# A one-core graph network kernel: the loads and the first of 16 batches in a new order, parameters worked out on GpSimd, the first neighbour product in single precision, and eight matmuls on zeros ahead of it

## The reference

```python
h = relu(bn(conv1d(xc, conv1_w, 0)))            # 1 tap, 128 -> 128 channels
h = bn(conv1d(h, conv2_w, 8))                   # 17 taps
x_conv = relu(h + xc)
s = x @ w_se.T + b_se                           # 3 columns
dist = sq[:, :, None] + sq[:, None, :] - 2 * einsum('bnd,bmd->bnm', s, s)
A = exp(-dist) * mask                           # mask is adj, 512 x 512
msg = relu(x @ w_msg.T + b_msg)
x_nmp = einsum('bnm,bmd->bnd', A, msg)          # the neighbour product
gi = concat([x_conv, x_nmp]) @ w_ih.T + b_ih;  gh = x @ w_hh.T + b_hh
r, z, n = sigmoid(..), sigmoid(..), tanh(gi_n + r * gh_n)
x = layernorm(x + (1 - z) * n + z * x)
```

## Time and profile before

| | us |
|---|---|
| median of 3 runs | 405.14 (403.12 to 405.31) |
| the profiled execution | 401.42 |
| its span | 399.1 |
| TensorE busy in the span | 374.6 (94%) |
| VectorE | 355.7 (89%) |
| ScalarE | 230.7 (58%) |
| GpSimd | 41.5 (10%) |

### The profile page before, as it was taken

One profiled execution on the slowest core, in us unless ns is written; L12 is line 12 of the kernel. 1 busy time (PEld: TensorE's weight loads), 2 busy tenths in 40 slices (PEclk: granted clock), 3 DMA queues, 4 the chain that ended last, 5 costly groups with the idle time before them and its releaser, 6 DMA issues.

```text
span 399.1 us, 7030 instructions
## 1 busy us (share of the span) xinstructions
PE 374.6 (94%) x2263; PEld 326.7 (82%) x2263; DVE 355.7 (89%) x731; ACT 230.7 (58%) x356; POOL 41.5 (10%) x46
## 2 busy tenths in 40 slices
PE   3589899999999999999999999999999999899995
PEld 2478689898979797989898898989797979688783
DVE  4988779999999999999999999999999999986646
ACT  4355456747565665666665667475656754654450
POOL 4500002110010101010101010100101060101013
PEclk9988889999999999999999999999999999999999
DMA  7627040504122221404040504040312204000100
GB/s 196 213 56 210 1 132 11 157 3 140 27 71 93 65 94 38 129 4 154 10 158 0 158 10 149 9 137 25 97 66 69 89 12 132 2 26 2 30 29 21
DMA packets 27305, 30.17 MB, mean 76 GB/s; under 512 B 3086, under 2 KB 16326, under 8 KB 27286
## 3 DMA queue, kind: packets, MB, share of 16 engines
q1 hardware_dynamic: 27256, 29.92, 24.5%
q10 hardware_dynamic: 30, 0.01, 0.0%
HBM read 24.84 MB, written 4.40 MB: 73 GB/s over the span
## 4 chain that ended last, share of the span: by engine, by line
PE 63%; DVE 21%; issue 10%; ACT 4%; DMA 1%; DVEq 0%; SPq 0%; POOLq 0%; ACTq 0%; POOL 0%
PE p_outer L602 14%; PE ring L602 13%; PE p_middle L602 8%; PE p_r L602 8%; PE p_z L602 8%; PE p_gi L602 7%; PE p_gh L602 4%; DVE sd_l L1121 3%; DVE dd L1107 2%; DVE sd L1116 2%; DVE st L1198 2%; DVE m_l L1130 2%; DVE n_l L1281 2%; DVE sd L1117 1%; ACT rows L840 1%
## 5 line engine op out<-in xcount | busy, mean ns | idle before, releaser
L602 PE MATMUL p_middle<-sd_h,w_h 128*128 128x256 f32 x192 | 56.7, 295 | 0.0
L1010 POOL TENSOR_TENSOR rs<-base,cst 128x5 f32<-128x5 f32 x16 | 20.0, 1250 | 332.7 <-DVE base L1209 332.7
L602 PE MATMUL p_middle<-sd_h,w_l 128*128 128x256 f32 x192 | 54.4, 283 | 0.0
L602 PE MATMUL p_middle<-sd_l,w_h 128*128 128x256 f32 x192 | 54.1, 282 | 0.0
L602 PE MATMUL p_outer<-dd_h,w_h 128*128 128x256 f32 x176 | 50.0, 284 | 2.5 <-issue 2.5
L865 ACT ACTIVATE am<-ring 128x512 f32<-128x512 f32 x64 | 37.9, 595 | 24.7 <-PE ring L602 24.3
L602 PE MATMUL p_outer<-dd_h,w_l 128*128 128x256 f32 x176 | 50.2, 285 | 0.0
L602 PE MATMUL p_outer<-dd_l,w_h 128*128 128x256 f32 x176 | 50.0, 284 | 0.0
L1136 DVE TENSOR_TENSOR am<-am,adj 128x512 f32<-128x512 f32 x64 | 40.9, 683 | 2.9 <-ACT am L865 2.9
L1252 DVE TENSOR_TENSOR am_l<-am,am_h 128x2048 fp32r<-128x2048 f32 x16 | 36.7, 2293 | 3.7 <-ACT am_h L914 3.7
L602 PEld LDWEIGHTS p_outer<-dd_h,w_h 128*128 128x128 f32 x176 | 34.0, 193 | 3.8 <-issue 3.2
(11 more groups left out here) (288 smaller groups left out, 969.7 us busy)
## 6 DMA issues: line engine op xcount, KB each, us to landing
adj<-adjT SPq DMA_DIRECT2D x64, 256.0 KB, 3.3
xin<-xT SPq DMA_DIRECT2D x17, 256.0 KB, 2.8
out<-yo SPq DMA_DIRECT2D x16, 256.0 KB, 2.2
gw<-g_w SPq DMA_DIRECT2D x2, 640.0 KB
wc<-w_c SPq DMA_DIRECT2D x2, 384.0 KB, 4.7
right<-left SPq DMA_DIRECT2D x14, 48.0 KB
wg<-w_ih SPq DMA_DIRECT2D x1, 384.0 KB, 5.8
wc<-w_c SPq DMA_DIRECT2D x1, 320.0 KB, 3.6
```

The lines of the kernel that those rows point to most:

```text
L602: return nc.tensor.matmul(out_, w, x, start=start, stop=stop, skip_group_check=True)
L1010: TT(rs[:], base[:], cst[:, C_MH:C_MH + CH + 1], ALU.pow).then_inc(s_rs, 1)
```

## The change

The pieces in front of the loop and step 0 become a function `first()` on TensorE, ScalarE and VectorE; the loop starts with step 1. What it does:

- SyncE's queue: the second batch's `xin` and the first third of `wc2` move ahead of `cst`; the loads of `bd` move from behind `xin` 2 to ahead of `bmsg`. ScalarE issues `vec`, `wc1` and `wrow` itself, ahead of its first instruction.
- GpSimd works out all of `prm` (10 small instructions; 14 were on VectorE, one on GpSimd). The two weight sums and `w4_l` go from GpSimd to VectorE. `right[1]` of the first pair is copied by a DMA instead of VectorE.
- TensorE runs eight matmuls of 128x512 on `right[0]`, just cleared, into `p_outer`, which is overwritten later.
- The neighbour product of batch 0 takes `am` and `m0` (relu of the messages, in the tile `zt`) as they are: 4 single-precision matmuls, no `am_h`, `am_l`, `m_h`, `m_l` for that batch.
- The four distance products of batch 0 have a bank each (`FIRST_D`). The identity is added to `sel1` on VectorE where it is read out of PSUM, not to `bd`.
- TensorE, ScalarE and VectorE have the same instructions otherwise, in another order.

```diff
             sp.dma_start(xin[:, 0, :], xT[0, :, :]).then_inc(s_x[0], 16)
-            sp.dma_start(wc1[:], w_c1[:, :]).then_inc(s_wc1d, 16)
-            sp.dma_start(vec[:], vecs[:, :]).then_inc(s_vec, 16)
+            sp.dma_start(xin[:, 1, :], xT[1, :, :]).then_inc(s_x[1], 16)
+            sp.dma_start(wc2[:, 0::3, :], w_c2[:, 0::3, :]).then_inc(s_w2d[0], 16)
             sp.dma_start(cst[:], consts[:, :]).then_inc(s_cst, 16)
...
+            def first():
+
+                pe.wait_ge(s_ready, 1)
+                for _ in range(8):
+                    mm(p_outer[:], right[0][:, 0:D], right[0][:])
+                pe.wait_ge(s_xh, 1); pe.wait_ge(s_w1s, 1)
+                mm(R_C1[:], wc1_h[:], x_h[0][:], True, False)
...
+                pe.wait_ge(s_left, 1); pe.wait_ge(s_right[0], 16); pe.wait_ge(s_h1, 1); pe.wait_ge(s_mt, 1)
+                for c in range(CH):
+                    mm(FIRST_D[c][:], left[:, D * c:D * c + D], right[0][:]).then_inc(s_d[c], 1)
...
+                pe.wait_ge(s_m0, 1); pe.wait_ge(s_mt, 2)
+                for c in range(CH):
+                    pe.wait_ge(s_am[c], 1)
+                    last = mm(R_NMP[:], m0[:, D * c:D * c + D], am[:, c, :], c == 0, c == CH - 1)
+                last.then_inc(s_nmp, 1)
...
+            def first():
+                act.dma_start(vec[:], vecs[:, :]).then_inc(s_vec, 16)
+                act.dma_start(wc1[:], w_c1[:, :]).then_inc(s_wc1d, 16)
+                act.dma_start(wrow[:, 64:128], w_rows[:, :]).then_inc(s_wrowd, 16)
+                z = Fixed(0)
+                x_high(0, z, 0)
+                x_high(0, z, 1)
+                act.wait_ge(s_zero, 3); act.wait_ge(s_prm, 5)
+                first_conv(z, 0)
...
+            pool.wait_ge(s_vec, 16); pool.wait_ge(s_zero, 1)
+            TS(prm[:, P_VE:P_VE + 2], vec[:, V_V1:V_V2 + 1:4], EPS, None, ALU.add).then_inc(s_prm, 1)
+            pool.wait_ge(s_prm, 1)
+            TT(prm[:, P_RS:P_RS + 2], prm[:, P_VE:P_VE + 2], half[:], ALU.pow).then_inc(s_prm, 1)
...
+            def first():
+                z = Fixed(0)
+                dve.wait_ge(s_wc1d, 16)
...
+                x_low(0, z, 1)
+                dve.wait_ge(s_brow, 32); dve.wait_ge(s_cst, 16)
+                TS(rowb[:], brow[:], cst[:, C_ROW:C_ROW + 1], cst[:, C_ROW + 1:C_ROW + 2], ALU.mult, ALU.add).then_inc(s_rowb, 1)
+                differences(z, 0)
...
+                TT(wsum[:, 0, 0:G3 - 1, :], wc2[:, 0:TAPS - 2:3, :], wc2[:, 2::3, :], ALU.add).then_inc(s_wsum, 1)
...
+                TT(w4_l[:], wc2[:, 2::3, :], full(w4_h[:]), ALU.subtract).then_inc(s_wlo, 1)
...
+                dve.wait_ge(s_bmsg, 16)
+                msg_sum(z, 0, FIRST_MSG)
...
+                TT(wsum[:, 1], wsum[:, 0], wc2[:, 1::3, :], ALU.subtract).then_inc(s_wsum, 1)
```

More of the change, by code:

```diff
@@ L216, in part @@
             return flat[0:rows, a:a + PAIRS * width].rearrange("p (j w) -> p j w", w=width)
-        sel1 = part(wc2, 0, 64, CC)
+        sel1 = [t[0:64, 0:4 * CC].rearrange("p (j w) -> p j w", w=CC) for t in (rt, nn)]
+        m0 = zt
         diag = part(wc2, 0, CC, CC)
@@ L479, in batches @@
         def batches(eng, step):
-            for b in (0, 1):
-                step(b, b, Fixed(b))
+            step(1, 1, Fixed(1))
             with eng.Fori(0, (B - 4) // 4) as i:
@@ L551, in _ @@
             sp.dma_start(xin[:, 2, :], xT[2, :, :]).then_inc(s_x[2], 16)
[L553 to L556, removed]
+            sp.wait_ge(s_left, 1)
+            sp.dma_start(full(right[1][64:64 + KD, :]), full(left[96:96 + KD, :])).then_inc(s_right[1], 16)
             for c in range(CH):
@@ L652, in transposes, with spread_rows @@
                 last.then_inc(s_t, 1)
-            def adjacency(stage):
+            def spread_rows():
                 sel = cst[0:64, C_SEL:C_SEL + CC]
[L657 to L667, removed]
-                            last = mm((p_gi, p_gh)[h][0:CC, CC * j:CC * j + CC], sel1[:, HP * h + j, :], sel)
-                        last.then_inc(s_acm, 1)
-                else:
-                    pe.wait_ge(s_ac, 2)
-                    for j in range(PAIRS):
-                        last = mm(p_middle[0:CC, j:j + 1], ac[0:CC, j, :], cst[0:CC, C_ONE:C_ONE + 1])
-                    last.then_inc(s_deg, 1)
+                pe.wait_ge(s_bdd, 32); pe.wait_ge(s_cst, 16); pe.wait_ge(s_val, 1)
+                for h in range(2):
+                    for j in range(HP):
+                        last = mm((p_gi, p_gh)[h][0:64, CC * j:CC * j + CC], bd[:, HP * h + j, :], sel)
+                    last.then_inc(s_sel1m, 1)
@@ new lines, in spread_columns, with degrees @@
+            def spread_columns():
+                sel = cst[0:64, C_SEL:C_SEL + CC]
+                pe.wait_ge(s_sel1, 2)
+                for h in range(2):
+                    for j in range(HP):
+                        last = mm((p_gi, p_gh)[h][0:CC, CC * j:CC * j + CC], sel1[h][:, j, :], sel)
+                    last.then_inc(s_acm, 1)
+            def degrees():
+                pe.wait_ge(s_ac, 2)
+                for j in range(PAIRS):
+                    last = mm(p_gi[0:CC, j:j + 1], ac[0:CC, j, :], cst[0:CC, C_ONE:C_ONE + 1])
+                last.then_inc(s_deg, 1)
@@ L932, in step @@
                     g_act.combined(act)
[L933 to L937 removed]
+                node_rows(n, -1)
+                conv_sums(n)
                 if more:
@@ L943, in step @@
                         g_act.channels(act, i)
-                after(act, s_cv, n(1)); after(act, s_gz, n(0))
-                A(c_h[:], cv[:], ACT.Relu).then_inc(s_ch, 1)
-                after(act, s_nmp, n(1)); after(act, s_gn, n(0))
-                A(n_h[:], R_NMP[:], ACT.Copy).then_inc(s_nh, 1)
+                conv_out(n)
+                neighbours(n)
                 if more:
                     exps(n, 1, 0)
-                after(act, s_gx, n(1)); after(act, s_tt, n(0))
-                A(gg[:], p_gh[:], ACT.Identity, bias=prm[:, P_HB:P_HB + 1], scale=0.5).then_inc(s_ghb, 1)
+                gate_n(n)
                 if more:
@@ L1279, in step @@
                     sums_low(n, 1)
[L1280 to L1292 removed]
+                neighbours_low(n)
+                conv_low(n)
+                normalise(q, n, -1, pair_of(b, v))
                 if more:
@@ L1303, in pair_of @@
                 return loop_pair[0] * 2 + (v - 1) // 2
-            for b in (0, 1):
-                step(b, b, Fixed(b))
+            first()
+            step(1, 1, Fixed(1))
             with dve.Fori(0, (B - 4) // 4) as i:
```

471 lines of the change are left out of this document (238 added, 233 removed).

## The result

The changed kernel takes 389.21 us (median of 4 runs, 387.48 to 390.19), the kernel before 405.23 beside it (4 runs, 403.12 to 406.61). The ratio is 0.9604, 95% interval 0.9550 to 0.9659: faster by 16.0 us. I had forecast 394.1 with a range of 390.5 to 399.0.

A forecast was written before the change was run, and what follows sets the result against it. With the loop unchanged and TensorE and VectorE nearly full, the second batch's earlier start was the whole effect. VectorE's terms, -4.3 - 0.6 - 4.2 + 3.4 - 4.8 - 0.1, gave -10.6, taken as -11: 405.14 to 394.1 us, range 390.5 to 399.

The forecast's parts named there:

- VectorE's shift is the smaller, so it decides: End of batch 0: VectorE's `gg` 11 us earlier, TensorE's step 1 13.1 earlier; the smaller shift reaches the end.
- The shift is the same for each: Whole time: the same 11 us come off the span, the profiled execution (401.42) and the median (405.14).
- The slow VectorE rows: VectorE, 9.75 to 16 us: three instructions slowed beside GpSimd's large ones return to 0.70 each, 4.3 us less.
- The rival that they stay slow: VectorE's 2 us instructions have another cause, such as loads, and stay slow: 401.5 us, chance 0.06.
- The instructions added and removed: VectorE in batch 0: 4.2 us less for instructions removed, 3.4 us more for those added.
- Idle time: VectorE from `rowb` to `gg`: walked 2.0 us of waits, took 3.0 instead of 7.8, 4.8 less.
- The start: VectorE's `rowb`, waiting for the load of `cst`, starts at 8.4 us instead of 8.51, 0.1 less.
- TensorE: TensorE in batch 0: step 1 starts at 40.7 us (-13.1), with a neighbour product of 3.3 us.
- none at the end: Matmuls on zeros before the first product: they may give TensorE 1.4 us, but nothing in the end time.
- Late load: Rival: `bmsg` or `cst` lands late and delays the first `mt` or `rowb`: 397 us, chance 0.12.
- slower: Rival: TensorE at half clock for the whole first batch, step 1 8.4 us later: 413.5 us, chance 0.04.
- Half clock: Rival: TensorE half-clock stretches after 26 us cost up to 4.8 us, 1 already in the sum: 398, chance 0.16.

The follow-up runs named there:

- e3: The changed kernel with the two weight sums and `w4_l` back on GpSimd: 391.71 us, ratio 0.977 to the kernel before.
- e4: The kernel before with only the two weight sums and `w4_l` moved from GpSimd to VectorE: 398.14 us, ratio 0.990.
- e1: The changed kernel without the eight matmuls on zeros: 389.90 us, ratio 0.972 to the kernel before.

## Why the prediction missed, point by point

- **The shift: "VectorE's shift is the smaller, so it decides" failed.** I had both walks: -13.1 us at TensorE's step 1, -11 at VectorE's `gg`, and took the second. Measured between the profiles: -13.5 and -12.9, and -13.5 at `gg` of batch 1 and -13.4 in the span. TensorE's shift reached the end, and VectorE's own was summed 1.9 us too small. This is 2.4 us of the miss; another 0.5 us lies outside the span (2.3 us before, 1.8 with the change), for which I had no term.
- **The level: "The shift is the same for each" failed too.** I took 11 us from the median of three, 405.14, though the profiled execution that I had read was 401.42. Beside the changed kernel the median of before was 405.23, 3.8 us above its profile, while the changed kernel's 389.21 was 1.7 above its own: 2.1 us more. 2.4 + 0.5 + 2.1 are the 5.0 us between 11.0 and 16.0. That before's four runs were long by half clock is likely from the later ones, but not shown. Against the later medians the difference is 10.7 us, and that it is near my 11 is luck: I walked from a profile that had half clock of its own in batch 0 (0.85 in the window of the earlier trace rows) and was 2.4 us longer than before's fastest run, and took the smaller shift.
- **The slow VectorE rows**, 4.3 us: right, by e3 and e4. The rival that they stay slow is out. (Of the batch norm's small instructions 13 were on VectorE, not 14.)
- **The instructions added and removed**: right. 0.82 for the 640 columns (0.8 predicted), 0.95, 0.58 for each `sel1` (0.6).
- **Idle time**: walked 2.0 us and measured 2.05, wait by wait (0.28 for 0.3, 0.17 for 0.5, 1.18 for 1.2). The 1 us of half clock on top wasn't there in either profile of the changed kernel.
- **The start**: `rowb` at 7.76, not 8.4; the line through two landings put `cst` 0.6 too late. The start and the 1 us of half clock make 1.6 of the 1.9 us by which `gg` came earlier than 42.0.
- **TensorE**: step 1 at 40.31 for 40.7; the product 3.03 us for 3.3. So this walk was right to 0.4 us, and it was the one to go by. The zeros cost nothing; in the time they bring nothing measurable, but "none at the end" was too little for the traces (0.9 us at `gg`, e1).
- **Late load, slower**: neither came; `mt` met `bmsg` without a wait, and the load took 4.8 us, not 6.7.
- **Half clock**: it was there, but as a property of the runs on both sides, and I priced it only for the changed kernel. The Trainium skill, TensorE: Matmul & The Clock Gate, Part 1, makes the slow clock the state of rest; the traces agree in direction (the first matmuls ran at 0.63 us, and where I looked the clock fell behind waits of 1.9 to 3 us or products of few columns), but the pair of profiles above shows that the same wait may or may not bring it, and in batch 0 of the changed kernel the degree products and the wait for `n_l` (0.36 us on TensorE) did not.

## What to carry to other kernels

Where two engines are both nearly full behind the changed part, don't take the smaller of their shifts by rule: find the engine from whose mark the distance to a later mark stays the same. Here the first profile of the change already told it. Before a predicted shift is taken from a median, ask which execution was profiled and what its mean clock was; where runs fall into groups, the shift belongs to the profiled one, and the range has to hold the groups. A short wait of TensorE that recurs costs more than its length: taking away 3.8 us of waits for `n_l` gave 5.9 us in the profile and 8.9 in the medians. Where VectorE's rows are three times their usual length, look at what GpSimd runs beside them before blaming the operands, and let each engine make first the operand that TensorE needs next.
